# A decoder's cross attention ending, the next layer's norms, rotary embedding and query and key split, made one block on Trainium2

## The reference, cut to what matters

```python
o  = LN(o) * g0 + beta0
o  = o + relu(o @ Wo + bo)
x  = x + LN(o) * g1 + beta1          # end of cross attention
xn = LN(x)                           # what grouped attention adds its result to
r  = xn / sqrt(mean(xn**2) + 1e-6) * norm1_w
r  = concat(even(r)*cos - odd(r)*sin, even(r)*sin + odd(r)*cos)   # rotary
q, k, v = r @ Wq, r @ Wk, r @ Wv     # 16 heads of 8 for q, 4 groups for k and v
```

## Time and profile before

| what | us |
|---|---|
| median of 3 runs | 1352.97 (1352.41 to 1353.62) |
| the profiled execution, its own time | 1364.93 |
| its span, first to last instruction | 1362.9 |
| busy PE / PE weight loads / DVE / ACT / POOL | 965.6 / 493.3 / 939.1 / 764.7 / 525.6 |
| mean granted PE clock | 0.723 of full |

### The profile page before, as it was taken

The page is one execution under the profiler, slowest core; times in us unless marked ns, Lnnn a source line. Parts: engine busy times, 40 slices in busy tenths (PEclk is TensorE's granted clock), DMA queues, the critical chain, the costliest instruction groups (busy, mean ns, idle before and its releaser), DMA issues. The chain is left out here.

```text
span 1362.9 us, 17675 instructions
## 1 busy us (share of the span) xinstructions
PE 965.6 (71%) x5593; PEld 493.3 (36%) x5593; DVE 939.1 (69%) x2073; ACT 764.7 (56%) x986; POOL 525.6 (39%) x418
## 2 busy tenths in 40 slices
PE   5886822579999736999275687778889776355275
PEld 2453221246666426999120011111111111034265
DVE  6676688468888263444579989999999996245401
ACT  4204513226666612444153699999999999921022
POOL 0000000200000004664156788888788878100264
PEclk9987965659999957999685556665555665666588
DMA  4001000112110005665244001000100000021145
GB/s 145 0 0 28 0 0 19 61 42 85 51 42 26 9 32 172 205 208 166 78 119 132 23 25 45 23 24 23 41 29 23 24 24 0 0 64 36 56 136 138
DMA packets 60155, 80.26 MB, mean 59 GB/s; under 512 B 14049, under 2 KB 37405, under 8 KB 59809
## 3 DMA queue, kind: packets, MB, share of 16 engines
q1 hardware_dynamic: 51072, 67.33, 16.2%
q0 software_dynamic: 3968, 8.13, 2.1%
q10 hardware_dynamic: 5024, 3.67, 0.8%
HBM read 63.56 MB, written 15.34 MB: 58 GB/s over the span
## 5 line engine op out<-in xcount | busy, mean ns | idle before, releaser
L2496 POOL TENSOR_TENSOR hb_t<-hb_t,hb_r 128x512 f32<-128x512 f32 x248 | 363.2, 1501 | 68.3 <-ACT hb_r L2312 66.8
L2509 DVE TENSOR_SCALAR hb_dpos<-hb_psR 128x1024 f32<-128x1024 f32 x128 | 155.8, 1218 | 19.8 <-PE hb_psR L2239 14.1
L2261 PE MATMUL hb_psO<-hb_t,ha_va 128*9 128x512 f32 x512 | 112.0, 974 | 67.6 <-ACT hb_t L2335 67.6
L2517 DVE SCALAR_TENSOR_TENSOR hb_t<-hb_psR,hb_dpos 128x1024 f32<-128x1024 f32 x128 | 155.2, 1212 | 0.4 <-PE hb_psR L2248 0.4
L2248 PE MATMUL hb_psR<-ha_q,ha_k 20*128 20x512 bf16 x256 | 120.9, 569 | 48.6 <-DVE hb_dpos L2509 48.5
L1843 ACT ACTIVATE ga_att<-ga_psB 128x512 f32<-128x512 f32 (+3 forms) x256 | 102.1, 453 | 74.7 <-PE ga_psB L1775 70.0
L1864 DVE TENSOR_REDUCE ga_nm<-ga_psA 128x1 f32<-128x128 f32 (+3 forms) x256 | 114.3, 485 | 35.8 <-PE ga_psA L1751 32.3
L2239 PE MATMUL hb_psR<-ha_q,ha_k 78*128 78x512 bf16 x256 | 122.0, 577 | 9.5 <-DMA ha_k<-hsx 3.6
L2335 ACT ACTIVATE hb_t<-hb_t 128x4096 f32<-128x4096 f32 x32 | 113.8, 3602 | 0.0
L2526 DVE SCALAR_TENSOR_TENSOR hb_r<-hb_t 128x1024 f32<-128x1024 f32 x64 | 104.7, 1636 | 0.0
L1625 POOL MEMSET ga_q<- 64x8192 bf16 x1 | 6.9, 6919 | 251.4 <-POOLq L1552 251.4
(11 more groups left out here) (469 smaller groups left out, 2211.8 us busy)
## 6 DMA issues: line engine op xcount, KB each, us to landing
m2x_e_w<-in_L_ffn_W_dram SPq DMA_DIRECT2D x78, 256.0 KB
m1x_e_w<-in_L_ffn_W_dram SPq DMA_DIRECT2D x23, 256.0 KB
ga_q<-qx SPq DMA_DIRECT2D x48, 96.0 KB
ha_q<-hqx SPq DMA_DIRECT2D x48, 96.0 KB
ha_k<-hkx SPq DMA_DIRECT2D x48, 96.0 KB
hy_fwd<-in_const_fwd_dram SPq DMA_DIRECT2D x1, 2048.0 KB
f_down<-in_L_ffn_W_dram ACTq DMA_DIRECT2D x4, 512.0 KB, 4.5
hsx<-hp_aparts SPq DMA_DIRECT2D x6, 288.0 KB, 4.1
```

Source lines behind the costliest of these rows:

```text
L2261: mm = pe.matmul(psO[32 * i:32 * i + VW, :], va[:, CH * (it // G) + c, HPG * (it % G) + i, :], t[:, (2 * it + form) % T_QUADS, 2 * half + ...
L2496: half_sum = pool.tensor_tensor(tt, tt, rr, ALU.add)
L2509: dve.tensor_scalar(dpos[:, n % 2, :], psR[:, dist_slot(n), :, :].rearrange("p i t -> p (i t)"), 0.0, None, ALU.max).then_inc(dpos_ready, 1)
L2517: dve.scalar_tensor_tensor(out=unit(t, n), in0=psR[:, side_slot(n), :, :].rearrange("p i t -> p (i t)"), scalar=CAP, in1=dpos[:, n % 2, :] ...
```

## The change

`cross_attention` keeps its main block; its parameters move into a class `CrossParams` (with two more columns, g0 and beta0, so 23 DMAs). The other blocks of the stretch ("xa_ln0", "xa_ln1", "ln3", "ga1", "ga_split", and a `recycle`) become one block, `prepare_queries`. Grouped attention's 8 parameter DMAs are issued in "ln2" behind cross attention's 23. Beside cross attention's main block POOL makes the rotary tables with the gain in them, adds beta1 to x, and clears the q and k buffers; DVE makes three casts there. In `prepare_queries`:

- Each of DVE, PE and ACT runs over the four batches phase by phase, in an order written out by hand. ACT normalises (`Identity` with scale and bias columns) in place of DVE, 64 calls of 128x128.
- The transposed copy for Wo takes gain and shift as columns in ACT's copy; PE adds the bias bo by a product with the identity; add and relu are one DVE operation.
- The RMS norm has no pass of its own: a second Sqrt and reciprocal of the variance give its scale. xn is written by ACT between other work.
- Rotary: two 128x512 products with the tables and two 128x256 sums a batch.
- The split has six items in place of eight: q of four batches, k of batch 0, k of batches 1 to 3 in one (96 rows). Each item is one store. The value products lie between the others; ACT copies them.
- SP stores items 0 and 1, waits for them, issues `q_load` of all four groups of batch 0, and then stores items 2 to 5. `q_load` has three DMAs for k in place of one, and source patterns that begin with the 8 rows of a head part in place of a repeat of 3; `kx` in DRAM is laid out to match, and `loaded[g]` counts 96 a load.

```diff
-        NPAR = 21
+        self.NPAR = 23
...
+def cross_attention(nc, cp, xnT, ident, pool, casts):
+        with s1.block() as block:
+            block.gpsimd(pool)
...
+                ch.link(dve.memset(vn[:, :, :, :], 0.0))
+                casts(dve, ch)
...
+def prepare_queries(nc, cp, x, xn, xnT, ident, rope, wqp, wk, wv, v, qx, kx, first_loads):
+    ITEMS = [("q", 0), ("k", 0), ("q", 1), ("q", 2), ("q", 3), ("k", 1)]
...
+            @block.sync
+            def _(sp):
+                def store(n):
+                    sp.wait_ge(lo_ready, n + 1)
...
+                    sp.dma_start(target, parts[0:rows(n), n, :, :]).then_inc(stored, 16)
+                store(0)
+                store(1)
+                sp.wait_ge(stored, 32)
+                first_loads(sp)
+                for n in range(2, len(ITEMS)):
+                    store(n)
+                sp.wait_ge(stored, 16 * len(ITEMS))
...
+                def add_output(b):
+                    if b >= 2:
+                        pe.wait_ge(summed, b - 1)
+                    pe.wait_ge(copied, b + 1)
+                    for c in range(CH):
+                        out = psW[:, b % 2, D * c:D * c + D]
+                        pe.matmul(out, ident[:, :], cp.bo[:, :], start=True, stop=False)
+                        mm = pe.matmul(out, hatT[...], w["Wo"][:, :], start=False, stop=True)
+                    mm.then_inc(projected, 1)
...
+                turn_hat(0)
+                for b in range(1, BATCH):
+                    turn_hat(b)
+                    add_output(b - 1)
+                add_output(BATCH - 1)
+                turn_rot(0)
+                for b in range(1, BATCH):
+                    turn_rot(b)
+                    project(b - 1)
+                    value(b - 1)
+                project(BATCH - 1)
+                value(BATCH - 1)
...
+                def normalise(n, b):
+                    act.wait_ge(scale_ready[n], b + 1)
+                    for g in range(CH * b, CH * b + CH):
+                        act.activation(hat[:, g, :], o[:, g, :], ACT.Identity, scale=rstd[:, n, 0, g:g + 1],
+                                       bias=shift[:, n, 0, g:g + 1]).then_inc(hat_ready[n], 1)
...
+                deviation(0, 0); deviation(0, 1); normalise(0, 0); deviation(0, 2); normalise(0, 1)
+                deviation(0, 3); copy_hat(0); normalise(0, 2); copy_hat(1); normalise(0, 3); copy_hat(2); copy_hat(3)
+                deviation(1, 0); deviation(1, 1); normalise(1, 0); deviation(1, 2); normalise(1, 1)
+                deviation(1, 3); normalise(1, 2); normalise(1, 3)
+                deviation(2, 0); deviation(2, 1); normalise_x(0, 1, r, r_ready); deviation(2, 2); normalise_x(1, 1, r, r_ready)
+                normalise_x(0, 0, xn, residual_ready); deviation(2, 3)
+                normalise_x(2, 1, r, r_ready); normalise_x(3, 1, r, r_ready)
+                copy_rot(0); normalise_x(1, 0, xn, residual_ready); copy_rot(1); high(0); high(1); middle(0)
+                copy_rot(2); middle(1); high(2); normalise_x(2, 0, xn, residual_ready); middle(2)
+                copy_rot(3); high(3); normalise_x(3, 0, xn, residual_ready); middle(3); high(4); high(5); middle(4); middle(5)
...
+                for b in range(1, BATCH):
+                    moments(0, b, o)
+                    scales(0, b - 1)
+                scales(0, BATCH - 1)
+                for b in range(BATCH):
+                    affine(b)
+                for b in range(BATCH):
+                    add_relu(b)
+                    moments(1, b, o)
+                    if b >= 1:
+                        scales(1, b - 1)
+                scales(1, BATCH - 1)
+                for b in range(BATCH):
+                    add_x(b)
+                    moments(2, b, x)
+                    if b >= 1:
+                        scales(2, b - 1)
+                scales(2, BATCH - 1)
+                for b in range(BATCH):
+                    rotate(b)
+                remainder(0); remainder(1); low(0); low(1); remainder(2); low(2); remainder(3); low(3)
+                remainder(4); remainder(5); low(4); low(5)
...
-    kx = nc.dram_tensor("kx", [BATCH, GROUPS, 3, DH, SEQ], BF16).ap()
+    kx = nc.dram_tensor("kx", [BATCH, GROUPS, DH, 3, SEQ], BF16).ap()
...
-                              qx[b, a, g, :, :, :].rearrange("(c d) i t -> c d (i t)", c=1).to_broadcast([3, DH, HPG * SEQ])
-            eng.dma_start(k[0:SPLIT, g, :], kx[b, g, :, :, :].rearrange("(a c) d t -> a (c d) t", a=1).to_broadcast([3, 3 * DH, SEQ]))
+                              qx[b, a, g, :, :, :].rearrange("(d c) i t -> d c (i t)", c=1).to_broadcast([DH, 3, HPG * SEQ])
+            for a in range(3):
+                eng.dma_start(k[3 * DH * a:3 * DH * a + 3 * DH, g, :], kx[b, g, :, :, :].rearrange("d a t -> (d a) t"))
...
+            def beside(pool):
+                pool.wait_ge(params, 16 * NPAR)
+                for a in range(2):
+                    for two in range(2):
+                        pool.tensor_tensor(rope[:, a, :, :, two], (cos, sin)[a ^ two][:, :, :], gain, ALU.mult)
+                pool.wait_ge(cp.params, 16 * cp.NPAR)
+                for b in range(BATCH):
+                    pool.tensor_tensor(quad, quad, over(cp.beta1[:, :], CH), ALU.add)
+                pool.memset(q[64:P, :, :, :], 0.0)
+                pool.memset(k[64:P, :, :], 1.0)
+            def first_loads(sp):
+                for g in range(GROUPS):
+                    q_load(sp, 0, g)
...
-            LOADS = 64
+            LOADS = 96
...
-                    for g in range(1, GROUPS):
-                        q_load(sp, 0, g)
```

More of the change, by code:

```diff
@@ L704, in _, with __init__, fetch @@
                     ch.link(dve.tensor_tensor(xs, ps[:, bank(b), :].rearrange("p (c d) -> p c d", c=CH), xs, ALU.add))
-def cross_attention(nc, A, x, xn, xnT, ident):
+class CrossParams:
+    def __init__(self, nc, st, A):
+        self.A = A
+        self.w = {k: st.sb(k, [P, D]) for k in ("Wq", "Wk1", "Wk2", "Wv1", "Wv2", "Wo")}
+        self.bo, self.g0, self.beta0, self.g1, self.beta1 = (st.sb(k, [P, D]) for k in ("bo", "g0", "beta0", "g1", "beta1"))
+        self.bqc, self.bk1, self.bk2, self.g0c, self.beta0c = (st.sb(k, [P, 1]) for k in ("bqc", "bk1", "bk2", "g0c", "beta0c"))
+        self.bv = st.sb("bv", [P, D])
+        self.hmask = st.sb("hmask", [P, HEADS])
+        self.pmask = st.sb("pmask", [P, D])
+        self.ctx = st.sb("ctx", [P, D])
+        self.o = st.sb("o", [P, TILES, D])
+        self.params = st.sem("params")
+        self.NPAR = 23
+    def fetch(self, nc, sp):
+        A = self.A
+        with nc.allow_non_contiguous_dma(reason="columns of parameters"):
+            for dst, src in [(self.w[k][:, :], A["L0_xattn_" + k]) for k in self.w] + [
+                    (dst[:, :], row(A["L0_xattn_" + k]).to_broadcast([P, D])) for dst, k in (
+                        (self.bo, "bo"), (self.g0, "g0"), (self.beta0, "beta0"), (self.g1, "g1"), (self.beta1, "beta1"))] + [
+                    (dst[:, :], column(A["L0_xattn_" + k])) for dst, k in (
+                        (self.bqc, "bq"), (self.bk1, "bk1"), (self.bk2, "bk2"), (self.g0c, "g0"), (self.beta0c, "beta0"))] + [
+                    (self.bv[CTX * n:CTX * n + CTX, :], row(A["L0_xattn_bv" + "12"[n % 2]]).to_broadcast([CTX, D])) for n in range(4)] + [
+                    (self.hmask[:, :], A["const_hmask"]), (self.pmask[:, :], A["const_pmask"]),
+                    (self.ctx[:, :], A["ctx_1024"].rearrange("b s d -> (b s) d"))]:
+                sp.dma_start(dst, src).then_inc(self.params, 16)
+def cross_attention(nc, cp, xnT, ident, pool, casts):
     KEYS = 2 * CTX
@@ L1628, in first_loads @@
[L1628 to L1636 removed]
+                              qx[b, a, g, :, :, :].rearrange("(d c) i t -> d c (i t)", c=1).to_broadcast([DH, 3, HPG * SEQ])).then_inc(loaded[g], 16)
@@ new lines, in q_load, with fetches, casts @@
+            for a in range(3):
+                eng.dma_start(k[3 * DH * a:3 * DH * a + 3 * DH, g, :],
+                              kx[b, g, :, :, :].rearrange("d a t -> (d a) t")).then_inc(loaded[g], 16)
+        with Stage(nc, "xa") as sx:
+            cp = CrossParams(nc, sx, A)
+            rope = sx.sb("rope", [P, 2, CH, D // 2, 2])
+            def fetches(sp):
+                cp.fetch(nc, sp)
+                fetch(sp)
+            layer_norm(nc, "ln2", x, xn, xnT, ident, sync=fetches)
+            def casts(dve, ch):
+                dve.wait_ge(params, 16 * NPAR)
+                ch.tick(dve.tensor_copy(mask_bf[:, :, :], mask[:, :, :]))
+                ch.tick(dve.tensor_copy(ident_bf[:, :], ident[:, :]))
+                ch.tick(dve.tensor_copy(wqp[:, :, :, :], wq[:, :].rearrange("p (g i d) -> p g d i", g=GROUPS, i=HPG)))
+            ones_ready = sx.sem("ones_ready")
+            rope_ready = sx.sem("rope_ready")
+            shift_ready = sx.sem("shift_ready")
+            def beside(pool):
+                pool.wait_ge(params, 16 * NPAR)
```

(16 more changed lines are left out.)

675 lines of the change are left out of this document (391 added, 284 removed).

## The result

The changed kernel takes 1328.95 us in the median of 4 runs (1327.23 to 1331.76), beside 1353.3 for the kernel before on the same chip. The ratio is 0.982 (0.980 to 0.983): **24.4 us less**, where 29.9 less was forecast. The profiled execution takes 1328.19, its span 1326.3. Busy are PE 968.3, DVE 923.5, ACT 777.5 and POOL 534.3, at a mean clock of 0.717.

The account below looks back on a forecast made before the run. It took the 104.5 us stretch as a chain through DVE, the new block as ended by SP at 74.1. Stretch 30.4 less, +3.1 and +0.5 lost, 3.1 gained: 1352.97 - 29.9 = 1323.1, range 1312 to 1336.

Parts of the forecast that it names:

- Ahead of the stretch, +3.1: Block before cross attention: SP's 10 added DMA issues hold it open, so cross attention's first PE work starts 3.1 us later.
- POOL beside cross attention, +0.5: Cross attention's main block: POOL's products and additions hold up DVE's first two-input operations, 0.5 us taken from 0 to 1.5.
- Compute of the new block, 57.4: New block: DVE's last subtraction of the split ends 57.4 us after the block's first DVE instruction.
- SP sets the end, 74.1: New block's end: 24 loads queue on SP ahead of the last four stores, so it ends at 74.1 us, not compute's 61.0.
- Three engines, 1.5 more: New block's end: if the 24 loads run on only three DMA engines, the stores end 1.5 us later.
- The wait for the maxima, -3.1: Start of grouped attention: PE's wait for the row maxima's DMA behind three groups' loads goes away, 3.1 us less.
- Steps of grouped attention: Later steps: six loads issued in place of four, 4.3 us in place of 2.9, cost nothing; cover 1.7 us.
- ACT the bound: New block: DVE's work moves to slower ACT, calls at 0.50 us and DVE waiting at phase turns, 1334.3 us; chance 0.19.
- Shorter end: New block's end: SP's issues are cheaper or hidden, 6.5 us earlier (1316.6) or 13.1 earlier (1310.0); chance 0.13.
- Slower: Grouped attention's steps: six loads ahead of `put_maxima` make each step wait, 1377 us at 1.6 an issue; chance 0.04.
- no change: New block: phases run one after another with whole-batch waits and the end is as late as before, about 1352; chance 0.02.

Follow-up runs that it names:

- the exchange of stores and loads: Against the changed kernel, only group 0's loads stand ahead of the late stores, groups 1 to 3 load at the next block's start: 1318.45 us.
- the experiment with both edits: Against the changed kernel, groups 1 to 3 load at the next block's start and q and k source patterns begin with 3 again: 1316.12 us, one run.
- the three edits: Against the changed kernel: only group 0 loaded ahead of the stores, 8 parameter DMAs in cross attention's main block, POOL's work there behind the first maximum: 1314.69 us.
- both kernels with three engines: Changed kernel with q and k source patterns beginning with 3 again: 1333.71 us; the same with groups 1 to 3 loaded in the next block: 1316.12 us.
- the first try with POOL: Against the changed kernel, POOL's memsets come first and its products and additions only behind cross attention's first maximum: 1326.13 us.

## Why the prediction was nearly right, and where it was off

The forecast was 1323.1 with a range of 1312 to 1336; 1328.95 lies inside, and it is faster, as said. Two terms were off by some 4 us each with opposite signs, and one was missing.

- *Ahead of the stretch, +3.1.* Measured 2.75, from 7.24 to 9.99 between the layer norm's transposes and cross attention's first PE work. The other 1.7 of the 4.45 are earlier still (those transposes are at 111.83 and 110.13). They are chance: in the 13 profiles the transposes start at 107.6 to 111.8, and at 108.4 in the second profile of the same kernel.
- *POOL beside cross attention, +0.5.* **This term failed**: measured 4.0, from 55.1 to 59.2 (58.2 in the second profile of the same kernel, so 3.1 there). I let two DVE operations fall into POOL's time and priced the wait at a part of one POOL operation. Both products waited, each for most of a POOL addition: 4.49 for the pair, 2.36 alone. With 0.4 by which the pair starts later, that is the 2.5 up to the first maximum. The casts were slowed too (2.3 for the three against 0.6), but this cost nothing here, since DVE then waited 3.1 for ACT's `xa_kT`. The other 1.5 are a consequence that I didn't look for: with the late start there comes one stretch at the low clock (0.50 of full, 1.2 GHz). In the six profiles where nothing of POOL's stands beside the casts and products it does not come.
- *Compute of the new block, 57.4.* Measured 55.5. By phases: `affine` from 7.3 (forecast 7.0), rotary from 35.25 (35.2). The split ends 1.9 earlier than said (and the recorded sum is itself 0.4 too low: 44.1 and three times 3.6 are 54.9, not 54.5). My low clock up to batch 0's k product, and full speed behind it, held in this profile; in the four with the later rise compute ends at 58.5 to 58.7. DVE was busy 47.6 and ACT 42.6 (forecast 50 and 40). A 128x128 ACT call with two columns takes 481 ns and 0.39 start to start, forecast 0.40; the Trainium skill, ScalarE: Activation LUTs, section What ACT_TABLE_LOAD costs, gives 93 ns for each such operand; the estimate from it and the earlier trace rows, 293 + 2 x 93 = 479, agrees.
- *SP sets the end, 74.1.* That it does was right, and is shown by the exchange of stores and loads. The size was 4.2 too high: 69.9. The loads begin at 48.3 (forecast 50.4), as the second store is issued 1.1 earlier and has landed after 1.8, not 2.6; a q load costs 0.69 and a k load 0.43. The bound of 0.47 that I had set aside for the plain pattern was the right one, so 24 loads took 14.3 in place of 17.3. From the first late store to the next block's PE work it is 7.2 (6.4): 0.54 to issue a q store and 1.19 for the one of 96 rows are more than I had allowed.
- *Three engines, 1.5 more.* Measured 7.3 in the profiles and 4.8 in the medians. I charged only the late drain, and from the first late store to the next block it is 8.7 against 7.2, the 1.5 said. Left out was that SP's issue gets slower too: 18.0 against 14.3. The other 2.1 are not the engines': the loads begin 50.5 after the block's first DVE instruction, not 48.3, by the late rise of the clock in this profile. So the patterns are worth 5.2 there.
- *The wait for the maxima, -3.1.* Measured 3.2, and the cause was right as to the loads on the DMA engines. In the kernel after they have all landed before the block begins; the experiment with both edits shows what happens where they haven't.
- *Steps of grouped attention.* Nothing, as said: six loads a step, and no step waits for them.
- *ACT the bound* (0.19). DVE waits for ACT 5.7 in the whole block, and 4.0 of it in the split, whose end decides nothing here. *Shorter end* (0.13): half of it came, by the k loads. *Slower* and *no change* did not.
- *What was missing.* At grouped attention's first exponential 29.3 us are gained, close to the 29.9, by errors that cancel: -4.2 at the block's end, +3.5 by POOL, +1.7 of chance from upstream. That it comes so close is luck: the second profile of the changed kernel has this exponential at 261.7, 34.5 earlier than the first profile of before. I took everything behind for a plain shift. By the first pair of profiles it gives back 3.5 (6.7 against the second profile of before, from 27.5 to 20.8 where the last router starts), which leads from 29.3 to 25.8, near the median's 24.4. How much of this is chance and how much belongs to the change isn't shown. The 12 us that I carried over from the profile of before to its median were in good part chance (7 in the last mixture); so the profiled execution, forecast at 1335.0, took 1328.19.

## What to carry to other kernels

Work that is moved to GpSimd "beside" a stage has to be laid against VectorE's instructions there, one by one, above all at the stage's start; a single wait that lets VectorE's first operations pass took 3.4 us off the block in the profile, though the median didn't tell it from a worse order. When a block's end is set by SyncE, count each issue and ask which of them the block's end needs: loads for later groups put ahead of the stores cost 10.5 us here, where the whole change won 24.4. And what a stage gains can be hidden behind it where later stages run at a clock that moves by some us from one profile to the next, so a forecast to the microsecond needs more than one profile of the stages that the change leaves alone.

## What the runs showed of the hardware

**VectorE and GpSimd shut each other out.** A cast of 0.29 took 4.99 while a GpSimd memset of 6.92 ran, and ended with it; the two 128x1024 products took 2.28 and 2.29 where they take 1.22, beside additions. But the 128x512 product of `xa_v` and the mask took 0.69, its usual time, beside a memset. The other way round, four additions on POOL took 5.92 beside these, 4.92 behind the first maximum. The two engines took turns, as the ends of the last addition (132.83) and of the second product (133.92) show: about 1.1 lie between them, the length of one product. The kernel after, each instruction by itself:

```profile
130.58 2.25 POOL L1908 TENSOR_TENSOR all_x<-all_x,xa_beta 128x512 f32<-128x512 f32 x1
131.63 2.29 DVE L874 TENSOR_TENSOR xa_kbd<-xa_kT,xa_hmask 128x1024 f32<-128x1024 f32 x1
```

The Trainium skill, SBUF — State Buffer, section SBUF: two separate sides, has this as an exclusive lock for a whole instruction, which a VectorE operation takes in a 2-port mode, or with two SBUF inputs, and then only against a GpSimd operation that reads SBUF. The products, the memset beside `xa_v` and the additions agree. So does the cast, if it runs in such a mode, which no run here shows. My prediction allowed for a delay and didn't lay the operations on one axis.

**One stretch at the low clock goes with a late start.** When DVE's products come late, PE pauses: 1.83 of 4 us busy in the first row below, then 0.57 granted. The profile taken again has PE at work there and the low clock at the block's end. A pause alone doesn't bring it: in the last row PE is busy for only 2.58 of 6 us and keeps 1.00. Cross attention's main block by windows, the kernel after, early in the block, then the profile taken again, at its end, then POOL's work behind the first maximum:

```profile
133.80:137.80 4.00, 1.83 (x6) 0.52 (x5) 3.29 (x6) 1.80 (x5) 4.00 (x1) 1.00 0.00 0
137.80:141.80 4.00, 4.00 (x7) 1.70 (x6) 1.80 (x3) 1.88 (x6) 3.75 (x2) 0.57 0.00 0
```

```profile
132.00:136.00 4.00, 3.69 (x9) 1.46 (x10) 2.72 (x5) 3.24 (x11) 4.00 (x1) 1.00 0.00 0
170.30:176.50 6.20, 4.21 (x20) 1.22 (x20) 0.85 (x3) 0.61 (x2) 0.00 (x0) 0.57 0.00 0
```

```profile
136.20:140.20 4.00, 3.48 (x8) 0.89 (x6) 2.64 (x7) 2.77 (x8) 3.94 (x5) 1.00 0.00 0
170.00:176.00 6.00, 2.58 (x20) 0.84 (x20) 1.34 (x6) 1.86 (x4) 0.00 (x0) 1.00 0.00 0
```

In 7 profiles POOL's work stands beside the casts or products, and each has exactly one such stretch, four of them 15 to 20 us after the block's start and three in its last 6; their blocks take 58.0 to 59.2. In the 6 profiles without (both of before, both with POOL behind the maximum, both of the three edits) the clock stays at 1.00 from 8 us on, and the block takes 55.1 to 55.8. The first maximum comes 12.4 to 13.5 after PE's first work in the seven, 10.7 to 11.4 in the six. Why it comes at one or the other place is open.

**The same in stages nobody touched.** The last 20 us before grouped attention's last exponential have a clock of 1.00 in 5 of 13 profiles (both of before, one of the kernel after, both kernels with three engines), and lie at 0.91 in one and at 0.83 in seven, 3.5 us longer; the kernel after has both. From memory attention's first DVE instruction to the next router's it takes 41.5 to 41.8 in four profiles (both of before, the first try with POOL, both edits at once) and 43.8 to 43.9 in nine. The products there show it, the kernel after and the first try with POOL, same stretch:

```profile
L3007 PE MATMUL mem_psA<-all_xn,mem_e 128*32 128x128 f32 x32 | 6.6, 397 | 4.7 <-DVE mem_e L3051 4.7
```

```profile
L3009 PE MATMUL mem_psA<-all_xn,mem_e 128*32 128x128 f32 x32 | 5.4, 337 | 4.7 <-DVE mem_e L3053 4.7
```

The data and the order of work are the same; the clock isn't. The one kernel that was profiled both short and long in grouped attention says that this goes with the execution. That both profiles of before are short in both stages and most of the others long may be chance or may come from where the stages start; no run here tells these apart, nor whether an earlier start itself brings the slower pattern. From `hp_eps` to POOL's first addition of `hb_t` it takes 61.8 and 62.5 in the profiles of before and 62.1 to 64.4 in the eleven others; this was not traced to a cause.
